# Moving two routers and a norm in the hand-written order of an attention and mixture-of-experts block

## What is computed

```python
h = _layernorm(x) * (1 + ca) + sa
x = x + ga * attention(h)            # causal softmax, 16 heads of 128
h = _layernorm(x) * (1 + cb) + sb
x = x + gb * ffn(h)

# ffn
t = h @ down_w + down_b                       # 256 -> 128
probs = softmax(h @ router_w + router_b - COST_LAMBDA * cost)
topv, topi = top_k(probs, 2); gate = softmax(topv)
out = sum over the two chosen experts of gate * (gelu(gelu(t * mask) @ w1 + b1) @ w2 + b2)
out = out + 0.1 * (gelu(gelu(t) @ shared_w1 + shared_b1) @ shared_w2 + shared_b2)
out = out @ up_w + up_b + (gelu(h) @ core_w + core_b)
```

## Time and profile before

| | |
|---|---|
| median of 3 runs | 814.39 us (811.27 to 814.85) |
| the profiled execution | 812.05 us, its span 810.0 us |
| PE busy | 784.7 us (97%) |
| PEld busy | 700.6 us (86%) |
| DVE busy | 679.5 us (84%) |
| ACT busy | 628.4 us (78%) |
| POOL busy | 441.2 us (54%) |

### The profile page before, as it was taken

The page is one execution under the profiler, slowest core; times in us unless marked ns, Lnnn a source line. Parts: engine busy times, 40 slices in busy tenths (PEclk is TensorE's granted clock), DMA queues, the critical chain, the costliest instruction groups (busy, mean ns, idle before and its releaser), DMA issues.

```text
span 810.0 us, 14461 instructions
## 1 busy us (share of the span) xinstructions
PE 784.7 (97%) x4806; PEld 700.6 (86%) x4806; DVE 679.5 (84%) x1649; ACT 628.4 (78%) x1417; POOL 441.2 (54%) x305
## 2 busy tenths in 40 slices
PE   7899899999999999999999999999999989989997
PEld 6789898999999999999999999999999767778786
DVE  4789998888888888888888888889898989887967
ACT  3787878877887788877778888877778968876974
POOL 2555365654456655445566544576545474577654
PEclk9999999999999999999999999999999999999999
DMA  7262233343222444322344332244332230111231
GB/s 264 64 171 68 63 90 93 91 104 86 66 66 66 101 108 108 83 66 66 72 104 106 91 92 66 66 97 115 94 76 60 64 105 34 67 58 66 69 102 53
DMA packets 47593, 70.54 MB, mean 87 GB/s; under 512 B 5536, under 2 KB 38464, under 8 KB 47392
## 3 DMA queue, kind: packets, MB, share of 16 engines
q1 hardware_dynamic: 47008, 68.81, 32.4%
q0 software_dynamic: 368, 0.81, 0.3%
q10 hardware_dynamic: 144, 0.00, 0.0%
HBM read 25.49 MB, written 2.17 MB: 34 GB/s over the span
## 4 chain that ended last, share of the span: by engine, by line
PE 64%; ACT 17%; DVE 11%; issue 5%; POOL 2%; DMA 1%; SPq 0%; DVEq 0%; POOLq 0%
PE M L732 10%; PE M L733 9%; PE M L731 9%; PE T L731 7%; PE T L733 7%; PE T L732 7%; PE S L731 5%; PE S L733 5%; PE S L732 5%; ACT PB L623 4%; ACT PB L672 3%; ACT pth L699 2%; DVE S L1135 2%; ACT qk L685 2%; ACT hh L665 1%
## 5 line engine op out<-in xcount | busy, mean ns | idle before, releaser
L623 ACT ACTIVATE PB<-S,nb 128x128 f32<-128x128 f32 (+3 forms) x256 | 133.9, 533 | 109.9 <-DVE nb L1135 109.9
L580 POOL TENSOR_TENSOR ptl<-ptl,pth 128x640 fp32r<-128x640 f32 x126 | 196.8, 1584 | 31.9 <-ACT pth L699 31.9
L573 POOL TENSOR_TENSOR X<-X,fb 128x512 f32<-128x512 f32 x64 | 83.1, 1299 | 239.5 <-DVE fb L1172 239.5
L672 ACT ACTIVATE PB<-PB,ri 128x256 f32<-128x256 f32 (+3 forms) x256 | 124.5, 580 | 6.4 <-DVE ri L1144 6.3
L1135 DVE CUSTOM_DVE_ANT_0 S<-S,cc 128x128 f32<-128x128 f32 (+3 forms) x256 | 117.6, 523 | 1.3 <-PE S L733 1.3
L1124 DVE TENSOR_TENSOR qk<-M,qk 128x512 fp32r<-128x512 f32 x108 | 74.6, 691 | 45.0 <-ACT qk L685 45.0
L1151 DVE STREAM_TRANSPOSE gab<-PB 128x256 f32<-128x256 f32 (+2 forms) x192 | 109.4, 623 | 0.0
L731 PE MATMUL S<-qk 128*128 128x128 f32 (+3 forms) x256 | 86.6, 338 | 4.6 <-DVE qk L1124 4.6
L699 ACT CAST pth<-ptl 128x640 fp32r<-128x640 f32 x128 | 87.8, 745 | 1.1 <-DMA ptl<-gab 1.1
L731 PE MATMUL M<-hh,W 128*128 128x512 f32 x222 | 86.7, 390 | 0.5 <-DVE hl L1110 0.5
L732 PE MATMUL M<-hl,W 128*128 128x512 f32 x222 | 86.5, 390 | 0.0
(11 more groups left out here) (255 smaller groups left out, 2410.7 us busy)
## 6 DMA issues: line engine op xcount, KB each, us to landing
ptl<-gab SPq DMA_DIRECT2D x256, 160.0 KB, 3.0
stage<-in_wat SPq DMA_DIRECT2D x16, 512.0 KB, 5.0
gab<-scw SPq DMA_DIRECT2D x16, 256.0 KB, 3.2
tmp<-scw SPq DMA_DIRECT2D x16, 256.0 KB, 3.6
X<-in_x SPq DMA_DIRECT2D x3, 512.0 KB, 8.3
stage<-in_wfa SPq DMA_DIRECT2D x3, 512.0 KB, 4.5
out<-X SPq DMA_DIRECT2D x3, 512.0 KB, 2.7
X<-in_wmod SPq DMA_DIRECT2D x1, 1024.0 KB, 11.8
```

Of the source, the lines that this page charges most:

```text
L573: pool.tensor_tensor(X[:, a:a + 512], X[:, a:a + 512], fb[:, c2 * 512:c2 * 512 + 512], ALU.add).then_inc(s_y, 1)
L580: pool.tensor_tensor(ptl[u % 2][:, s], ptl[u % 2][:, s].bitcast(F32), pth[u % 2][:, s].bitcast(F32), ALU.subtract).then_inc(s_pl, 1)
L623: ins = act.activation(PB[:, P_OFF[i]:P_OFF[i] + w], PS[bk][:, a:a + w], ACT.Exp, bias=nb[:, i:i + 1], scale=-1.0, accum_out=sm[:, i:i + 1])
L672: act.activation(p, p, ACT.Copy, scale=ri[:, i:i + 1]).then_inc(s_P3, 1)
```

## The change

- r 1 moves from behind chunk 5 of batch 0 to ahead of z 62, at the end of the attention plan. Its later steps stay where they are.
- Steps 6 to 9 of router 0 move behind ("dn", 0) and ("z", 61).
- The split of weight piece 22 moves from chunk 4 to chunk 5.
- ("nm", 6, 1), the second half of the norm of batch 2, moves ahead of ("dn", 1) behind chunk 11.
- r 2 moves from chunk 6 of batch 1 to chunk 15 of batch 0; its steps 1 and 2 to chunk 18; its exponentials to chunks 19 and 20 of batch 0 and 0 and 1 of batch 1; steps 3 to 14 from chunks 14 to 18 of batch 1 to chunks 4 to 8.
- So that the sums of one router can lie beside those of the one before, L gets two places in `rt`, and k = 0 is counted by a semaphore of its own, `s_rl`; step 1 waits for it and for the end of the router before, and raises `s_rt` by two.

```diff
     plan += [("S", u), ("wo", u // 2 - 2, 1), ("v", u // 2, 1), ("ex", u), ("ri", u), ("r", 0), ("rs", 0, 1),
-             ("rs", 0, 2), ("pt", u - 1), ("ra",), ("wx", u // 2 - 2, 1), ("b1",)] + [("rs", 0, k) for k in range(3, 10)] + [
-             ("dn", 0), ("z", u - 2)]
-    return plan + [("norm", u), ("ty", u), ("tr", u), ("z", u - 1), ("ld", 22)]
+             ("rs", 0, 2), ("pt", u - 1), ("ra",), ("wx", u // 2 - 2, 1), ("b1",)] + [("rs", 0, k) for k in range(3, 6)] + [
+             ("dn", 0), ("z", u - 2)] + [("rs", 0, k) for k in range(6, 10)]
+    return plan + [("norm", u), ("ty", u), ("tr", u), ("r", 1), ("z", u - 1), ("ld", 22)]
...
-        first, exps, rest = steps
-        put(*first, ("r", b))
-        put(first[0], first[1] + 1, ("rs", b, 1), ("rs", b, 2))
+        sums, first, exps, rest = steps
+        if sums:
+            put(*sums, ("r", b))
+        put(*first, ("rs", b, 1), ("rs", b, 2))
         for c in range(4):
-            put(exps[0], exps[1] + c, ("rp", b, c))
+            put(exps[0] + (exps[1] + c) // (NC + 1), (exps[1] + c) % (NC + 1), ("rp", b, c))
...
-    put(0, 4, ("wx", last - 1, 1), ("wh", 22))
+    put(0, 4, ("wx", last - 1, 1))
+    put(0, 5, ("wh", 22))
...
-    put(0, 11, ("dn", 1), ("nm", 6, 1))
+    put(0, 11, ("nm", 6, 1), ("dn", 1))
...
-    router(1, ((0, 5), (0, 6), (0, (11, 11, 11, 12, 12, 14, 14, 15, 15, 15, 16, 16))), (0, 19))
+    router(1, (None, (0, 6), (0, 6), (0, (11, 11, 11, 12, 12, 14, 14, 15, 15, 15, 16, 16))), (0, 19))
...
-    router(2, ((1, 6), (1, 8), (1, (14, 14, 14, 15, 15, 16, 16, 17, 17, 17, 18, 18))), (2, 0))
-    router(3, ((2, 4), (2, 5), (2, (11, 11, 11, 12, 12, 14, 14, 15, 15, 15, 16, 16))), (2, 19))
+    router(2, ((0, 15), (0, 18), (0, 19), (1, (4, 4, 4, 6, 6, 6, 6, 7, 7, 7, 8, 8))), (2, 0))
+    router(3, ((2, 4), (2, 5), (2, 5), (2, (11, 11, 11, 12, 12, 14, 14, 15, 15, 15, 16, 16))), (2, 19))
...
-                L, e0, pr = rt[:, 0:32], rt[:, 32:64], rt[:, 64:96]
+                L, e0, pr = rt[:, 192 * (b % 2):192 * (b % 2) + 32], rt[:, 32:64], rt[:, 64:96]
...
-                    if b:
-                        v.wait_ge(s_rt, 15 * b)
+                    if b >= 2:
+                        v.wait_ge(s_rt, 15 * b - 15)
...
-                    if k:
+                    if k == 0:
+                        router(ev, b, k).then_inc(s_rl, 1)
+                    elif k == 1:
+                        v.wait_ge(s_rl, b + 1)
+                        if b:
+                            v.wait_ge(s_rt, 15 * b)
+                        router(ev, b, k).then_inc(s_rt, 2)
+                    else:
                         v.wait_ge(s_rt, 15 * b + k)
-                    router(ev, b, k).then_inc(s_rt, 1)
+                        router(ev, b, k).then_inc(s_rt, 1)
```

More of the change, by code:

```diff
@@ L312, in build @@
         s_id = sem("s_id")
-        s_ri, s_P3, s_rt, s_st_ = sem("s_ri"), sem("s_P3"), sem("s_rt"), sem("s_st_")
+        s_ri, s_P3, s_rt, s_st_, s_rl = sem("s_ri"), sem("s_P3"), sem("s_rt"), sem("s_st_"), sem("s_rl")
         s_ob, s_d0 = sem("s_ob"), sem("s_d0")
```

## The result

The changed kernel takes 817.20 us in the median of 11 runs (813.85 to 821.69), the kernel before 814.39 us (811.27 to 816.85). The ratio is 1.0042, with a 95% interval of 1.0026 to 1.0057: slower, by 0.42%, where I had forecast 0.1% faster with a range of up to 817.5. (The ratios on record are not the quotients of the two medians, which here would be 1.0035.) Sign and cause are wrong although the median lies inside the range.

The account below looks back on a forecast made before the run. TensorE, by far the busiest engine, was taken to bound the kernel, with waits after 630 us. Terms 3.8 - 0.9 - 1.7 + 0.3 - 2.1 = -0.6 us on the 814.39 us median gave 813.8, lowered to 813.5; range 809.5 to 817.5.

Parts of the forecast that it names:

- r 1 in the gap before z 62, and its bank: End of attention: r 1 fits the gap, but wo (30, 0) starts 3.05 us late on its bank; 0.7 late after.
- rival (c): The clock falls at 640 us too, during the wait before wo (30, 0): 1.7 us on top, 814 to 815.5; chance 0.15.
- The norm: Before h2 (2, 0): with the norm ahead of two gelus, the 1.02 us wait goes and TensorE is 0.5 early.
- r 2's wait: At r 2's new place, behind chunk 15 of batch 0: TensorE waits 2.9 us for h2 (2, 1)'s low half.
- Swallows router 1's gains and losses alike: Claim that r 2 starts 2.5 us late at its new place whatever was won or lost before.
- r 2's own cost: From r 2's new place to dta 0: r 2 itself adds 1.70 us; dta 0 taken as 3.8 late, clock included.
- The allowance for the clock here: From r 2 to dta 0: a clock fall costs up to 1.7 us, half hidden by a wait, so 0.5 to 0.9.
- Router 2's steps at chunks 4 to 8: Batch 1: about 3.5 us of steps on a nearly full VectorE cost 0 to 1.5 us, taken as 0.3.
- the sign of being wrong: TensorE waiting over 1 us between 691 and 705 us, in batch 1, would show the prediction wrong.
- Rival (b): VectorE falls behind in chunks 4 to 8 of batch 1: 4.5 us of waiting, +3.6 us or 819 with a dip; chance 0.10.
- The wait before batch 2: Before batch 2's first w1: the 2.07 us wait goes, since router 2's steps no longer stand ahead of dn 2.
- Sum: Whole change: 3.8 - 0.9 - 1.7 + 0.3 - 2.1 = -0.6 us, between -3 and +2.5.

Follow-up runs that it names:

- e1: The changed kernel with router 2 and the norm put back, leaving the moves of r 1, router 0's steps and piece 22; 816.28 us, 1.0028 of before.
- e4: The changed kernel with steps 3 to 14 of router 2 back at chunks 14 to 18 of batch 1; 813.64 us, 0.9991 of before.
- e5: As e4, but r 2 behind chunk 20 of batch 0, its steps 1 and 2 and exponentials at chunks 1 to 5 of batch 1; 815.95 us.
- e3: The changed kernel with r 1's sums in bank 2, so that wo (30, 0) takes bank 1 as before; 815.39 us, 1.0021 of before.
- e2: The changed kernel with router 0, r 1 and piece 22 put back, leaving the norm and router 2 moves; 815.96 us, 1.0013 of before.
- e10: The changed kernel with small matmuls on zeros in the waits, 50 ahead of wo (30, 0) and 40 ahead of r 2; 814.86 us, 1.0013 of before.
- e12: As e11, but router 0, r 1 and piece 22 where they were before the change; 810.60 us, 0.9957 of before.
- e7: As e5, with r 1's sums in bank 2; 814.23 us, 1.0014 of before.
- e8: As e5, but r 1, steps 6 to 9 of router 0 and piece 22 where they were before the change; 814.97 us, 1.0010 of before.
- e11: As e9, with 40 small matmuls on zeros ahead of r 2; 810.94 us, 0.9959 of before.
- e9: The changed kernel with the edits of e3 and e4 together; 812.85 us, 0.9985 of before.

## Why the prediction was wrong

- **r 1 in the gap before z 62, and its bank.** Right in mechanism and size: the idle of VectorE ahead of dn 0 was 1.02 us (forecast 1.0), the wait before wo (30, 0) 3.18 us (3.05), no wait before z 63. The term was short by the clock: I gave the fall near 640 to rival (c), and it came, in the profile of the change, of e1, e4 and e5. It made w1 6 late by 2.55 us instead of 1.15; VectorE's own lateness covered all but 0.3 of it at wo (31, 0), where (c) had 0.5 to 1.7.
- **The norm.** Right: the 1.02 us wait went (e1, without it, has it).
- **r 2's wait.** Right, 2.66 us (2.9 forecast). "Swallows router 1's gains and losses alike" was wrong, as e3 shows, and contradicts the step ahead of it, which carries 0.7 us through the same queue.
- **r 2's own cost.** I moved 1.70 us. At 1.2 GHz it took 681.66 - 678.26 = 3.4 us, since its starts lie 0.21 us apart instead of 0.11. The allowance for the clock here, 0.5 to 0.9, was too small: 4.3 late at w1 16 and 5.05 at dt against 3.8.
- **Router 2's steps at chunks 4 to 8: the step that failed.** I put them at 0.3 us within 0 to 1.5. They cost 3.4 us of waiting and 3.6 us in the medians (change against e4); in this profile 2.5 us of slow clock stand behind the waits. That part was luck of the execution: e2, e3 and e10 have the same two waits (2.15 to 2.22 and 1.22 us), and their clock stays full there. I counted 2 us of lag as free, and relied on VectorE starting the stretch caught up; but I added up only what the change adds, and not all that VectorE had to do there, which filled it already. The count itself used a wrong distance, as does the description of the kernel before. The code has TensorE wait for `s_gl` >= n - 3, that is for the low half of chunk n - 4: four chunks, and 5.6 us where I had 4.2, of which some 3.6 would be free by my own reckoning. But so much was never free: in the trace of before it was 1.2 us, as shown above. The same distance is why the waits stand just behind the stretch of 691 to 705 us that I had named as the sign of being wrong. And the steps took 5.8 us, not 3.5. Rival (b) had the mechanism, place and price (4.5 us of waiting); I gave it 0.10 and it was the main case, nearest in the medians to its 3.6 us without a further clock fall.
- **The wait before batch 2.** Right that it goes, wrong in why: e4 and e12 show that it goes with r 2 and its pow operations early and the other steps late. That made the risk in the step above needless.
- **Sum.** In the terms of the sum, in this profile: 5.05 for 3.8, then -2.85 for the -2.6 that come back, 3.9 for 0.3, and +0.3 for -2.1. With the failed step alone taken back, e4 lies 0.5 us below before, where the rest of the sum, -0.9, had it. That is partly luck: e4's trace has 1.7 and 3.4 us of missing clock at 640 and 675 us, more than I had allowed, and its first w1 of batch 2 is 0.8 us late against the trace of before.
- **Clock or waiting.** In the 35 executions of the kernel before, 1 us more of missing clock goes with some 0.6 us more of span. By that, an estimate, the 1.7 us of missing clock between e4 and the change are 1 us of the 3.5 us between the medians of their spans (811.8 and 815.3), and 2.5 us are waiting.

## What to carry to other kernels

When an in-order engine is full, moving short steps to an earlier place moves a wait instead of removing it; sum all of that engine's work over the stretch, then the lag its consumer allows. Moving an event also changes which buffer it and its successors get: walk the rotation for every user behind it, in each place that you try. And look first at which engine made the old wait: here, by the rows, four operations on GpSimd more than the twelve on VectorE. A short step beside another engine's long operation can last as long as what is left of that operation, so such chains belong where that engine is idle.

## What the runs showed of the hardware

In every trace here, from 625 us on, a wait of TensorE of 2.66 to 3.19 us that was left idle was followed by 3 to 10 us at 1.2 GHz, with 1.7 (e7) to 5.1 us (e8) of missing clock. The waits of 2.7 us had r 2's matmuls of 16 columns behind them, those of 3.2 us had matmuls of 256 columns. Waits of 1.9 to 2.1 us were not followed by a fall, and the pair of 2.2 and 1.2 us was in one trace of four. At 1.2 GHz the 16-column matmuls of r 2 start 0.21 us apart instead of 0.11. The Trainium skill, TensorE: Matmul & The Clock Gate, Part 1, has activity as what keeps the clock up, and e10 and e11 agree: matmuls on zeros in the wait brought 2.3 us (change to e10) and 1.9 us (e9 to e11) back, though the real work waited as long. I had not expected that filling a wait with useless work would be the largest gain left.
